# Tanh sums of single-unit blocks: one piece moved from ScalarE to GpSimd (last batch: every second block), the rest to VectorE

## The reference, cut to what matters

```
txt_proj  = ctx @ Ws                                  # 4 x 77 x 256
feat_proj = layernorm(x) @ W                          # 4 x 1024 x 256
h   = tanh(txt_proj[:, None, :, :] + feat_proj[:, :, None, :] + b)
rho = h @ w ; rho += (1 - mask) * -1e30 ; att = softmax(rho)
w_s = tanh((att @ ctx) . Wcw + bcw) ; b_s = tanh((att @ ctx) . Wcb + bcb)
x   = x + w_s * layernorm(x) + b_s
n   = layernorm(x)
probs = softmax(n @ gate) ; scores, idx = top_k(probs by expert, 512 tokens)
x   = x + scatter_add(scores * (gelu(n[idx] @ W1 + b1) @ W2 + b2)) + gelu(n @ Ws1 + bs1) @ Ws2 + bs2
```

## Time and profile before

| what | value |
|---|---|
| median of 3 runs | 893.86 us (893.48 to 893.88) |
| profiled execution, first to last instruction (span) | 892.1 us, mean granted TensorE clock 0.992 |
| between its span and the median of the runs | 1.8 us |
| busy: TensorE, VectorE, ScalarE, GpSimd | 801.3, 708.7, 767.8, 307.6 us |
| first and last large tanh (L995) start at | 19.6 us, 614.7 us |
| large tanh: 103 of 128x4096, 34 of 128x3584 | 366.6 us, 108.9 us busy |
| direct pieces of 128x512: 57 | 39.9 us busy |

### The profile page before, as it was taken

How to read it: one execution, slowest core, us unless ns; L and a number is a source line. 1 busy time by engine, 2 the same in 40 slices (tenths; PEclk the granted TensorE clock), 3 DMA queues, 4 the chain that set the end, 5 groups by cost and what they waited for, 6 DMA issues and landing times.

```text
span 892.1 us, 14125 instructions
## 1 busy us (share of the span) xinstructions
PE 801.3 (90%) x5385; PEld 472.7 (53%) x5385; DVE 708.7 (79%) x1405; ACT 767.8 (86%) x601; POOL 307.6 (34%) x537
## 2 busy tenths in 40 slices
PE   7975679569998999999999999999988999999996
PEld 5321123124443444445454455545766899999986
DVE  5899889898989689988878995894887877676641
ACT  3989999999999999999999999997753677676672
POOL 3310540615543007674002740052203145555424
PEclk9899999999999999999999999999999999999998
DMA  8000000000001000200000010002202365544513
GB/s 267 19 1 0 1 1 1 1 24 15 10 9 40 1 1 25 71 2 1 24 1 1 25 48 1 24 1 89 77 24 78 98 181 142 136 106 132 137 20 41
DMA packets 32406, 41.82 MB, mean 47 GB/s; under 512 B 2365, under 2 KB 29011, under 8 KB 32339
## 3 DMA queue, kind: packets, MB, share of 16 engines
q1 hardware_dynamic: 26083, 32.49, 10.9%
q0 software_dynamic: 6144, 8.39, 5.7%
q10 hardware_dynamic: 112, 0.04, 0.0%
HBM read 28.33 MB, written 12.58 MB: 46 GB/s over the span
## 4 chain that ended last, share of the span: by engine, by line
PE 39%; ACT 38%; issue 11%; DVE 9%; POOL 1%; DMA 0%; POOLq 0%; ACTq 0%; DVEq 0%
ACT z L995 31%; PE bank L914 10%; PE bank L937 9%; PE bank L787 7%; DVE z L1372 4%; PE bank L829 3%; PE bank L844 3%; ACT z L991 2%; ACT u L1038 2%; PE bank L763 2%; PE bank L715 1%; PE bank L952 1%; PE bank L817 1%; ACT L1038 1%; PE bank L888 1%
## 5 line engine op out<-in xcount | busy, mean ns | idle before, releaser
L995 ACT ACTIVATE z<-z 128x4096 f32<-128x4096 f32 (+5 forms) x157 | 520.9, 3364 | 4.6 <-DVE z L1372 4.4
L1372 DVE TENSOR_SCALAR z<-feat,txt_bias 128x1024 f32<-128x1024 f32 (+1 forms) x722 | 421.9, 656 | 36.5 <-PE bank L787 35.6
L787 PE MATMUL bank<-z,window 128*32 128x512 f32 x2464 | 304.9, 604 | 64.0 <-ACT z L995 62.5
L787 PEld LDWEIGHTS bank<-z,window 128*32 128x32 f32 x2464 | 70.0, 110 | 249.7 <-issue 134.1
L844 PE MATMUL bank<-ws_sb,u 128*128 128x256 f32 x512 | 126.3, 387 | 5.6 <-ACT u L1038 5.6
L844 PEld LDWEIGHTS bank<-ws_sb,u 128*128 128x128 f32 x512 | 92.2, 189 | 41.1 <-issue 19.8
L829 PE MATMUL bank<-tr,ws_s 128*128 128x512 f32 x384 | 107.9, 417 | 0.0
L914 PE MATMUL bank<-xg_s,w_s 128*128 128x512 f32 x384 | 99.5, 397 | 0.2 <-DVE xg_s L1672 0.2
L937 PEld LDWEIGHTS bank<-w_s,hid_s 128*128 128x128 f32 x672 | 86.3, 188 | 4.0
L937 PE MATMUL bank<-w_s,hid_s 128*128 128x256 f32 x672 | 88.2, 280 | 0.0
L1074 ACT ACTIVATE hid<-bank,vec 128x512 f32<-128x512 f32 x64 | 44.2, 690 | 49.3 <-PE bank L914 49.2
(11 more groups left out here) (264 smaller groups left out, 750.4 us busy)
## 6 DMA issues: line engine op xcount, KB each, us to landing
w_raw<-in_L_ffn_W_dram SPq DMA_DIRECT2D x16, 1024.0 KB, 5.6
x_ring<-in_x_dram SPq DMA_DIRECT2D x8, 512.0 KB, 7.9
xn_dram<-xn SPq DMA_DIRECT2D x8, 512.0 KB, 2.9
out_dram<-x_ring SPq DMA_DIRECT2D x8, 512.0 KB, 3.2
u<-in_L_ffn_Ws_dram SPq DMA_DIRECT2D x1, 1024.0 KB, 11.0
ws_sb<-in_L_ffn_Ws_dram SPq DMA_DIRECT2D x1, 1024.0 KB, 13.7
xg<-xn_dram,idx POOLq DMA_INDIRECT x32, 4.1
out_dram<-y,idx POOLq DMA_INDIRECT x32, 3.9
```

Source lines behind the costliest of these rows:

```text
L787: ins = e.matmul(sums[v][32 * r:32 * r + 32, :], window[:, c, 31 - k:63 - k], z[:, n % ZB, at_piece:at_piece + TOK], start=(v, r) not in b ...
L995: e.activation(part, part, ACT.Tanh).then_inc(signal(*step), 1)
L1372: ins = e.tensor_scalar(z[:, n % ZB, i * width:(i + 1) * width], feat_of(units, c), bias_of(units, t, c), None, ALU.add)
```

## The change

In single-unit blocks a new step `help(n)` is written into the order directly behind `add(n)`. On GpSimd it makes the last of the summed pieces. `tanh(n)` waits for it as well as for `add(n)`. Which blocks are helped is given by `helped_pieces`: blocks 2 to 7 and 31 to 38, and of blocks 129 to 156 those with an even number. These are 6 + 8 + 14 = 28 helps. The direct pieces of single-unit blocks fall by one in blocks 2 to 7 and to none from block 31 on. This removes 6 + 8 + 28 = 42 direct pieces of 128x512 from ScalarE, and its large ACTIVATE grows by 512 columns in each of these blocks. VectorE sums what is left: the same number of pieces as before in helped blocks, one more in the 14 blocks of the last batch that are not helped. Pair blocks are unchanged.

```
-FIRST_DIRECT = (4, 3, 3, 3, 2, 2, 2, 2)
-DIRECT_EVERY = (15, 1)
+FIRST_DIRECT = (4, 3, 2, 2, 1, 1, 1, 1)
+FIRST_HELPED, HELP_EVERY = 2, 2
+DIRECT_EVERY = 15
...
     if len(units) > 1:
-        return 1 if n % DIRECT_EVERY[0] == 0 and len(pieces) > 2 else 0
-    return 1 if n % DIRECT_EVERY[1] == 0 else 0
+        return 1 if n % DIRECT_EVERY == 0 and len(pieces) > 2 else 0
+    return 0
+
+
+def helped_pieces(n, units, pieces, UPB):
+
+    if len(units) > 1 or n < FIRST_HELPED:
+        return 0
+    return 1 if units[0] < UPB or n % HELP_EVERY == 0 else 0
...
     def add(n):
         order.append(("add", n))
+        if helped_pieces(n, blocks[n][0], blocks[n][2], UPB):
+            order.append(("help", n))
...
                     e.wait_ge(*done("add", n))
+                    if helped_pieces(n, units, pieces, UPB):
+                        e.wait_ge(*done("help", n))
                     e.activation(part, part, ACT.Tanh).then_inc(signal(*step), 1)
...
+                elif kind == "help":
+                    n, = args
+                    units, k, pieces = blocks[n]
+                    last = len(pieces) - direct_pieces(n, units, pieces)
+                    r, t, c = pieces[last - 1]
+                    for v in units:
+                        e.wait_ge(*done("feat", v, c))
+                    e.wait_ge(*done("txt_bias", 1 if units[0] >= UPB else 0, c))
+                    if n >= ZB:
+                        e.wait_ge(*done("rho", n - ZB))
+                    e.tensor_scalar(z[:, n % ZB, (last - 1) * TOK:last * TOK], feat_of(units, c), bias_of(units, t, c),
+                                    None, ALU.add).then_inc(signal(*step), 1)
...
-                    for i in range(len(pieces) - direct_pieces(n, units, pieces)):
+                    for i in range(len(pieces) - direct_pieces(n, units, pieces) - helped_pieces(n, units, pieces, UPB)):
```

## The result

The change makes the kernel slower. Its median is 912.67 us (912.31 to 913.38, 4 runs) against 893.85 us (893.48 to 893.88) before: +18.8 us, ratio 1.0212 with a 95% interval of 1.0197 to 1.0226. The direction was forecast. The size was not: +7.3 us was expected, and 912.67 is outside the range. The profiled execution has a span of 910.6 us, 18.5 more than before.

What follows compares the result with a forecast made beforehand. ScalarE sets the pace until the last batch, where TensorE is hardly behind. 2.7 + 2.4 + 3.5 - 2.5 + 1.2 = +7.3 us: span 899.4, median 1.8 above it, so 901.2 us; 8-in-10 range 896.8 to 906.0.

Steps and rivals of the forecast that it cites:

- Step a: Start-up: three helps ahead of x_norm(1) delay it and all behind it, +2.7 us (bounds 2.1 and 3.6).
- 3 x 0.9: Start-up: three helps of 0.9 us each on GpSimd make x_norm(1) end 2.7 us later.
- TensorE's wait grown to about 4 us: Sign that the forecast is right: TensorE's wait at its turn for x_norm(1) grows from 1.5 to about 4 us.
- Step b: Blocks 31 to 38: seven helps take time from VectorE, the tight engine there, +2.4 us (bounds -0.7 and +5).
- Step c: Block 130: the help stands behind y_scale(5), ScalarE waits 3.9 us, +3.5 us (bounds 2.5 and 4.4).
- Step d: Blocks 131 to 156: ScalarE saves 4.9 us, of which at most 2.7 can be won back, -2.5 us.
- I cost both at nothing: Blocks 131 to 156: VectorE's 14 extra pieces (5.6 us) and 14 collisions (6.3) count as zero, covered by its waits.
- Step e: Unit 6's second norm: help(154) stands ahead of y_scale(6), so TensorE waits at its turn, +1.2 us.
- Whole-instruction collision: Rival, all helps: each stops VectorE for its full 0.9 to 1.2 us; +12.2 us, 906.1 us, chance 0.12.
- my 0.45: VectorE's loss per help from collision: 0.45 us, twice the 0.23 us per GpSimd instruction of about 256 columns.
- What a help costs: Length of a help on GpSimd, scaled from its 128x256 TENSOR_SCALARs: 0.9 us, bounds 0.7 and 1.2; VectorE loses 0.45 us.

Runs made afterwards that it cites:

- the two-operation kernel: The whole change with each help issued as feat x 1.0 + bias (two operations, two pointers), still 128x512; 912.52 us, ratio 1.0207.
- the kernel without extras: Against the kernel before, only the last batch changed: helps in even blocks, odd blocks keep their direct piece; 908.48 us, ratio 1.0160.
- The kernel without helps: Against the kernel before, only the last batch changed: no helps or direct pieces, VectorE adds every piece; 893.88 us, ratio 0.9996.

## Why the prediction was right in direction and wrong in size

Between the +7.3 us forecast and the +18.8 measured lie 11.5 us. The steps account for 10.9 of them: a 4.0, b 0.4, c 1.7, d 6.0, e -1.2.

- **Step a, start-up: +2.7 forecast, +6.7 measured.** The mechanism held: with no help ahead of x_norm(1) the loss shrank to 0.7. The term "3 x 0.9" was wrong twice. Three helps took 5.49 us (1.83 each), above even the upper bound of 3.6. And the sum had no term for TensorE's clock: the turn's wait grew from 1.53 to 6.3 us, and behind it 2.6 us went to the 1.2 GHz level. In the two-operation kernel the missing term is as large as the delay itself: the three helps took the 2.7 us forecast, and block 8 was 5.2 late. "TensorE's wait grown to about 4 us" was in my own list; what follows such a wait I did not ask.
- **Step b, blocks 31 to 38: +2.4 forecast, +2.8 measured.** Right, though its term was not. In the kernel with only these blocks changed 14 adds beside x_norm and three helps took 8.30 us, in the kernel before, beside x_norm alone, 5.99:

```profile
127.49 8.30 DVE L1396 TENSOR_SCALAR z<-feat,txt_bias 128x512 f32<-128x512 f32 x14
```

```profile
127.39 5.99 DVE L1372 TENSOR_SCALAR z<-feat,txt_bias 128x512 f32<-128x512 f32 x14
```

  A help cost VectorE 2.31 / 3 = 0.77 us, not 0.45, and more of it than the 0.8 us that I allowed fell into its waits. Two errors cancelled, so the close number was luck. (The upper bound was given as +5 here and as 5.5 under the rival, from the same terms; 5.5 is the sum.)
- **Step c, block 130: +3.5 forecast, about +5.2 measured** (the shift goes from 9.1 to 14.4 in the trace, and by 5.1 in the kernel without extras). The place, the releaser and the queued gelu were as forecast. Too small was the help's length, 2.36 us for 0.9: that is the whole difference between the wait of 3.9 us that I reckoned and the 5.37 measured. The chain ahead of it took 6.95 us, before 6.86.
- **Step d, blocks 131 to 156: -2.5 forecast, about +3.5 measured** (14.4 at block 130 to 17.9 at 156). This is where the prediction failed most. "I cost both at nothing", for VectorE's extra pieces and for the collisions, was wrong on both counts. One starved help took 2.9 us at block 138. ScalarE waited for VectorE at 145 and 151 by 2.1 and 2.2 us, and at 136 by 0.7. The kernel without helps has such waits too (1.7 us at 145, 1.3 at 136), and the one with helps and no extra pieces as well (1.4 at 145, 0.5 at 151), so load and helps each make a part. With 28 extra pieces and no helps the net was 0.0 us, where this step had a gain of 2.5. It can go further: the same step costs some 7 us more when the starved help is that of 154, 2.6 of it by the clock.
- **Step e, unit 6's second norm: +1.2 forecast, 0 measured.** Help(154) ended at 617.61, 18.7 us later than my 598.9, when the whole kernel was 18.3 late. But the chain behind it, for which I took the 13.6 us of before, ran from 617.58 to 628.60, in 11.0: its large part took 2.17 us instead of 3.73. So it ended 0.6 us ahead of the turn at 629.21. The mechanism I named is real, though: it appears with 4.2 to 4.9 us of TensorE's wait as soon as help(154) is starved.
- **The rivals.** "Whole-instruction collision" came nearest in size, +12.2, and fell short too. Its rule, of the Trainium skill, SBUF — State Buffer, section Who interferes with whom, is that in VectorE's two-port modes the port pair is held for a whole instruction while the other engine is fully blocked. The starved helps would fit a lock that VectorE's chained adds hand on to each other; no run here shows the lock itself. Helps that get in stretch two adds, whose records last 0.47 us undisturbed (one begins every 0.40), to 0.8 or 0.9 us each: VectorE loses 0.77 us, about half of the help's 1.56. The measured price on VectorE's side lies between my 0.45 and that rival's 0.9 to 1.2; on GpSimd's side, where the rule makes the help wait, I had allowed 0.3 us and the runs showed up to 9.

Two steps of the prediction failed. The first is "I cost both at nothing" in step d, with -2.5 us forecast and +3.5 measured, the largest miss. The second is "What a help costs", on which a, b and c stood: I took the row of 0.55 us, GpSimd's 128x256 TENSOR_SCALAR with two operations, and scaled it to an instruction of twice the width with one operation. The width was scaled well, for the two-operation help takes 0.77 us where I had 0.88; it is the form that doubled it, to 1.56 alone and 2.15 in the mean. The groups by form could have warned that the row was a best case, with a mean of 1.08 us for the same instruction in the kernel before:

```profile
L1134 POOL TENSOR_SCALAR xn<-x_ring,y_ry,offset 128x256 f32<-128x256 f32 x32 | 34.3, 1083 | 0.8
```

That mean mixes company: 0.56 us beside no adds, 0.92 beside 128x512 adds, 1.41 beside those of 128x1024. Twice it is 2.17, near the 2.15 measured, but by accident, since nothing in it knows of the form. Length alone does not carry the miss either: with helps of 0.77 us the kernel still lost 18.6, as another help was starved. And a term was missing altogether, TensorE's clock behind a new wait: 2.0 us of step a in the changed kernel.

## What to carry to other kernels

Before giving a spare engine a piece of work, ask what stands behind that piece in its queue: here the three helps ahead of x_norm(1) made 6.0 of 18.8 us, and those of blocks 130 and 138 another 5.2 and 2.9. Price an operation by its group's mean in the company that it will have, not by its best row, and price its form (single or double operation) as well as its size. Count a wait of TensorE as more than its length, since the work behind it may run at half clock; and where an engine has some room, as VectorE had, giving it the work can beat giving it to one whose instructions its own hold up (+0.0 against +9.2 us in the last batch).

## What the hardware did that I had not expected

- GpSimd's 128x512 add takes 1.56 us with one operation and 0.77 us with two (feat x 1.0 + bias), both beside no adds. Why, and whether the operation or the pointer counts, no run here shows.
- A help that began inside a run of VectorE's adds at 0.40 us each was held until the run ended, once or twice in 7 of the traces here (7.2 to 7.9 us at block 138, 9.2 to 10.8 us at block 154). Others that began in or near such runs got in after one to four adds, and a few near the start were held to the end of a run that was short (3.1 and 3.3 us at block 7). What decides is open: start times relative to the add in progress showed no rule, and the spread of 897.39 to 904.59 us of one kernel suggests that it can differ between executions.
- TensorE idle for 1.75 us kept its full clock. After 3.37 us of idle time it ran the next 16 matmuls of rho in 3.48 instead of 1.93 us (granted clock 0.53), and after 4.73 us the turn and the 8 matmuls behind it took 5.6 instead of 2.9 us (granted clock 0.50).
